# Two narrow attentions of a decoder joined into one pipeline of sixteen sequences

## The reference

```
self:   q = rope(x@Wq)  k = rope(x@Wk)  v = x@Wv     (8 key/value heads, each used by 4 heads)
        s = q.k, causal;  attn = softmax(s/4);  ctx = attn@v
        ctx = swapaxes(ctx,-2,-1).reshape(b,t,512);  x = layernorm(x + ctx@Wo)
cross:  q = axial_rope(x@Wq)  k,v = split(ctx_1024@Wkv);  k = axial_rope(k)     (32 key/value heads)
        attn = softmax(q.k/4);  x = layernorm(x + attn@v@Wout + bout)
```

## Time and profile before

| | us |
|---|---|
| median of 3 runs (4342.74 to 4356.64) | 4351.02 |
| the profiled execution | 4323.99 |
| its span, from first to last instruction | 4322.0 |
| mean granted TensorE clock, share of 2.4 GHz | 0.931 |
| TensorE matmul busy | 3714.3 (86%) |
| VectorE busy | 1918.8 (44%) |
| ScalarE busy | 1308.8 (30%) |
| self attention, narrow | from 2036 to about 2808 |
| cross attention, narrow | from about 2808 to about 3616 |

### The profile page before, as it was taken

The page is one execution under the profiler, slowest core; times in us unless marked ns, Lnnn a source line. Parts: engine busy times, 40 slices in busy tenths (PEclk is TensorE's granted clock), DMA queues, the critical chain, the costliest instruction groups (busy, mean ns, idle before and its releaser), DMA issues. The chain is left out here.

```text
span 4322.0 us, 60181 instructions
## 1 busy us (share of the span) xinstructions
PE 3714.3 (86%) x20058; PEld 2564.1 (59%) x20059; DVE 1918.8 (44%) x6611; ACT 1308.8 (30%) x2941; POOL 279.3 (6%) x304
## 2 busy tenths in 40 slices
PE   7899999899999998894688887768777886799996
PEld 7667777677777776542455554434444443577775
DVE  4334433344443443214454545545555555543435
ACT  1233322333333333411232333224333344221121
POOL 2231000030000000413000000000000000000000
PEclk8999999999999999897788999879999998899998
DMA  6511111131111111444000000010000001100001
GB/s 222 176 41 53 44 39 39 48 135 42 44 41 41 46 44 68 151 136 127 1 1 2 2 1 1 1 39 3 4 3 6 4 1 40 30 10 19 10 19 39
DMA packets 83735, 191.45 MB, mean 44 GB/s; under 512 B 22416, under 2 KB 27792, under 8 KB 82456
## 3 DMA queue, kind: packets, MB, share of 16 engines
q0 software_dynamic: 31360, 94.52, 7.1%
q1 hardware_dynamic: 52192, 94.53, 6.3%
HBM read 138.56 MB, written 50.47 MB: 44 GB/s over the span
## 5 line engine op out<-in xcount | busy, mean ns | idle before, releaser
L1696 ACT ACTIVATE probsT_c<-bank 128x512 f32<-128x512 f32 x256 | 147.5, 596 | 369.6 <-PE bank L1559 369.6
L1786 DVE TENSOR_REDUCE mx_y<-bank 128x2 f32<-128x512 f32 x288 | 185.9, 688 | 153.2 <-PE bank L1534 151.9
L1696 ACT ACTIVATE probsT_y<-bank 128x512 f32<-128x512 f32 x256 | 147.7, 596 | 312.6 <-PE bank L1552 310.0
L446 PE MATMUL bank<-wo_s,work_s 128*128 128x512 f32 x512 | 228.9, 598 | 7.1 <-ACT work_s L478 3.8
L446 PE MATMUL bank<-wo_x,work_x 128*128 128x512 f32 x512 | 227.2, 594 | 5.1 <-ACT work_x L478 3.8
L478 ACT ACTIVATE work_s<-bank 128x512 f32<-128x512 f32 (+1 forms) x224 | 104.2, 465 | 355.7 <-PE bank L435 174.4
L478 ACT ACTIVATE work_x<-bank 128x256 f32<-128x256 f32 (+1 forms) x240 | 109.6, 460 | 322.9 <-PE bank L435 188.6
L583 DVE CUSTOM_DVE_ANT_0 work_x<-bank,work_x 128x256 f32<-128x256 f32 x256 | 97.8, 420 | 221.0 <-issue 221.0
L524 ACT ACTIVATE work_x<-work_x 128x256 f32<-128x256 f32 x256 | 128.3, 502 | 195.9 <-DVE work_x L588 195.9
L583 DVE CUSTOM_DVE_ANT_0 work_s<-bank,const 128x128 f32<-128x128 f32 (+1 forms) x256 | 80.8, 353 | 214.3 <-issue 214.3
L1534 PE MATMUL bank<-kT_c,qT_c 64*128 64x256 f32 x576 | 91.2, 403 | 97.3 <-DVEq L1797 96.3
(11 more groups left out here) (416 smaller groups left out, 8195.4 us busy)
## 6 DMA issues: line engine op xcount, KB each, us to landing
wq_lo_s<-wq_lo_s POOLq DMA_DIRECT2D x64, 512.0 KB, 3.6
wq_lo_x<-wq_lo_x POOLq DMA_DIRECT2D x64, 512.0 KB, 3.5
expert_rows<-table_zero SPq DMA_DIRECT2D x20, 512.0 KB, 14.1
work_m<-expert_rows SPq DMA_DIRECT2D x40, 256.0 KB, 2.6
expert_products<-work_m POOLq DMA_DIRECT2D x40, 256.0 KB, 2.7
expert_table<-table_zero SPq DMA_DIRECT2D x16, 512.0 KB, 13.7
weights_m<-expert_table SPq DMA_DIRECT2D x4, 2048.0 KB, 9.8
ug_rows<-in_L_ffn_W_gate SPq DMA_DIRECT2D x9, 512.0 KB, 3.9
```

Of the source, the lines that this page charges most:

```text
L446: last = pe.matmul(out[t][:, :], oT[:, h, t * P:(t + 1) * P], wo[:, h, :], start=(h == 0), stop=(h == H - 1), skip_group_check=True)
L1696: act.activation(probsT[:, h % PTS, :], scoreT[h % 2][:, :], ACT.Exp, scale=SCALE)\
L1786: dve.tensor_reduce(mx[:, :, h], b[:, :].rearrange("p (t k) -> p t k", t=TILES), AX.X, ALU.max)\
```

## The change

The two calls become one. The 16 items are sequences 0 to 7 of the self attention and then 0 to 7 of the cross attention, written out without a loop (`ITEMS = 16`, `step(n, at)`).

- The finishing of item n-1 lies in the steps of item n: h0, h2 in step 0; h1, h3 in step 1; hT0, hT1 in step 3; out0 in step 8; out1 in step 9; bias, statistics, root and normalising in steps 10 to 13 (`norm_stage`). There is no tail between items.
- Item n+1 is prepared in steps 0 to 13 (k in 0 and 1, q in 4 and 5, v in 11 and 12), `xT` and `ctxT` of item n+2 in steps 14 and 15. `x_static` is gone: x is turned out of `x_all`. First scores lie in steps 8 to 15, two pairs each.
- The split is now high, low, high (or high, high, low): 48 rows of 64. The keys have ones in rows 48 and 49, and the negative maxima of the queries' rows (high and low) are written into rows 48 and 49 of `qT` by 8 small DMAs per item out of `negT` (negA for pairs 0 to 7, negB for 8 to 15). Second scores contract 50 rows; the matmuls with `select` are gone.
- For self, first scores of the first tile take 128 keys instead of 256, second scores of the second half 128 queries instead of 256, and the causal mask is added to the first scores by a bf16 matmul as well (2 more of 256 columns per pair). Maxima are one reduction per pair for both kinds: 128x768 for self, 128x1024 for cross.
- One exponential per pair (128x768 and 128x1024) instead of two of 128x512.
- Values of four heads at a time, in all four groups of 32 columns, at even steps; one bank for their result, three for `prep`.
- The cross weights are loaded on GpSimd's queue while self items run.

```diff
-        self.bank = [ctx.enter_context(nc.psum_tensor(f"bank{i}", [P, 512], FP32)) for i in range(8)]
+        self.banks = [ctx.enter_context(nc.psum_tensor(f"bank{i}", [P, 2, 512], FP32)) for i in range(4)]
+        self.bank = [self.banks[i // 2][:, i % 2, :] for i in range(8)]
...
+    def step(n, at):
+        f = n - 1 if n >= 1 else None
+        g = n + 1 if n + 1 < ITEMS else None
+        e = n + 2 if n + 2 < ITEMS else None
+        a, b = [], []
+        if f is not None:
+            a += {0: ["h0", "h2"], 1: ["h1", "h3"]}.get(at, [])
+            b += {3: ["hT0", "hT1"] if cross(f) else [], 8: ["out0"], 9: ["out1"]}.get(at, [])
+        a, b = [(x, f) for x in a], [(x, f) for x in b]
+        if at == 2:
+            a.append(("negB", n))
+        if g is not None:
+            whole = [x for x in ("kT02", "kT03", "kT12", "kT13") if cross(g)]
+            a += [(x, g) for x in {3: ["kT01"] + whole[0:1], 4: ["q0"] + whole[1:2], 5: ["kT11"] + whole[2:3],
+                                   6: ["qT00", "qT01"], 7: ["qT03", "qT10"], 10: ["qT12"], 11: ["v0"], 12: ["qT13"],
+                                   13: ["negA"]}.get(at, [])]
+            b += [(x, g) for x in {0: ["k0"], 1: ["k1"], 2: ["kT00"], 4: ["kT10"], 5: whole[3:4] + ["q1"], 6: ["qT02"],
+                                   7: ["qT11"], 12: ["v1"]}.get(at, [])]
+            if at >= 8:
+                a.insert(0, (2 * (at - 8), g))
+                b.insert(0, (2 * (at - 8) + 1, g))
...
+            for n in range(ITEMS):
+                for i, name in enumerate(("negA", "negB")):
+                    sp.wait_ge(s["prep_act"], uses.nth[name, n])
+                    for r in range(2):
+                        for l in range(2):
+                            row, at = 64 * r + ROWS + l, 16 * l + 8 * r
+                            sp.dma_start(qT[row:row + 1, n % 2, 8 * i:8 * i + 8, :].bitcast(FP32), negT[at:at + 8, i, :].bitcast(FP32))\
+                              .then_inc(s[f"{name}_there"], 16)
...
+            def second_scores(n, pair):
+                if pair % 8 == 0:
+                    pe.wait_ge(s["negA_there" if pair == 0 else "negB_there"], 64 * (n + 1))
+                pe.wait_ge(s["exp_ready"], n * PAIRS + pair)
+                for k in range(TILES):
+                    for h in (2 * pair, 2 * pair + 1):
+                        keys = kT[half(h, ROWS + 2), n % 2, key_block(n, h), k * P:(k + 1) * P]
+                        q0 = 0 if cross(n) else k * P
+                        last = pe.matmul(scoreT[:, h % 2, k * SEQ:(k + 1) * SEQ - q0], keys,
+                                         qT[half(h, ROWS + 2), n % 2, pair, q0:SEQ],
+                                         start=(k == 0), stop=cross(n), skip_group_check=True)
...
+            def values(n, quad):
...
+                for k in range(TILES):
+                    q0 = 0 if cross(n) else k * P
                     for i in range(4):
+                        h = 4 * quad + i
+                        kv = h if cross(n) else h // 4
+                        last = pe.matmul(hbank[VW * i:VW * (i + 1), col + q0:col + SEQ],
+                                         v[:, n % 2, k, VP * kv:VP * kv + VW],
...
+            for n in range(ITEMS):
+                for at in range(PAIRS):
+                    second_scores(n, at)
+                    early, late = step(n, at)
+                    for name, item in early:
+                        emit(name, item)
+                    if at == 0 and n >= 1:
+                        values(n - 1, 7)
+                    elif at >= 2 and at % 2 == 0:
+                        values(n, at // 2 - 1)
+                    for name, item in late:
+                        emit(name, item)
+            values(ITEMS - 1, 7)
+            for name, n in after:
+                emit(name, n)
```

More of the change, by code:

```diff
@@ L1301 @@
 NH, VW = 32, 32
[L1304 to L1340, removed]
@@ new lines, in read, with four, project @@
+            def read(name, n):
+                pe.wait_ge(s[f"prep_{uses.engine[name, n]}"], uses.nth[name, n])
+            def four(b, block):
+                for i in range(4):
+                    last = pe.transpose(b[:, P * i:P * (i + 1)], block(i), chip.ident)
+                return last
+            def project(b, src, t, w, width, chunks):
+                for cc in range(chunks):
+                    last = pe.matmul(b[:, 0:width], src[:, cc, t * P:(t + 1) * P], w[:, cc, :],
+                                     start=(cc == 0), stop=(cc == chunks - 1))
+                return last
@@ new lines, in finish @@
+                    last = four(b, lambda j: heads_n[:, j % 2, (2 * i + j // 2) * P:(2 * i + j // 2 + 1) * P])
+                else:
+                    if i == 0:
+                        read("hT1" if cross(n) else "h3", n)
+                        pe.wait_ge(s["wo_cross_loaded" if cross(n) else "wo_loaded"], 16)
+                    for j in range(DC):
+                        if cross(n):
+                            a = headsT[:, j, i * P:(i + 1) * P]
+                        else:
+                            a = heads_n[:, j % 2, 2 * i * P + j // 2:2 * (i + 1) * P:2]
+                        last = pe.matmul(b[:, :], a, wo[:, j, :], start=(j == 0), stop=(j == DC - 1))
@@ new lines, in keep_heads @@
+            def keep_heads(n, quad):
+                turn_ = n * 8 + quad
+                act.wait_ge(s["values_ready"], 4 * (turn_ + 1))
+                if n >= 1:
+                    act.wait_ge(s["prep_ready"], uses.ready["h2" if quad < 4 else "h3", n - 1])
+                col = turn_ % 2 * SEQ
+                copy(heads[:, quad, :], hbank[:, col:col + SEQ]).then_inc(s["heads_copied"], 1)
+            act.wait_ge(s["consts_ready"], 1)
+            for name, n in mine(before):
+                evacuate(name, n)
@@ new lines, in _ @@
+            for n in range(ITEMS):
+                for at in range(PAIRS):
+                    early, late = step(n, at)
+                    for name, item in early:
+                        do(name, item)
+                    if n >= 1 and at in (10, 11, 12, 13):
+                        norm_stage(at - 10, n - 1)
+                    for name, item in late:
+                        do(name, item)
+            for name, n in after:
+                do(name, n)
+            for part in range(4):
+                norm_stage(part, ITEMS - 1)
```

731 lines of the change are left out of this document (322 added, 409 removed).

## The result

| | before | after |
|---|---|---|
| median of 4 runs, us | 4352.95 (4342.74 to 4356.64) | 3948.45 (3942.04 to 3958.78) |
| profiled execution, us | 4323.99 | 3946.09 |
| mean granted clock | 0.931 | 0.933 |
| first second scores to the last output projection, us | 1504.2 | 1107.6 |

The ratio is 0.908 (95% interval 0.905 to 0.910). The change made the kernel 404 us faster; I had forecast 303. The sign was right, and 3948 lies inside the stated range of 3935 to 4150, but only because that range was stretched to take in the rival in which the clock stays up (3936).

The account below looks back on a forecast made before the run. It took TensorE's work and its waits, for maxima in late steps, as the bound. Prologue 70, self items of 74.5, cross items of 78.9 and the end summed to 1275 against 1577 us: 4048, own range 3990 to 4100, stated 3935 to 4150.

Parts of the forecast that it names:

- the rival in which the clock stays up: No clock loss in late steps: 16 x 7 = 112 us less than forecast, 3936; chance 0.18.
- the end of the bounds that I took: Values of four heads: 0.98 us (all side by side) to 1.96 (two by two); 0.98 taken.
- The estimate of 1.2 us: Time of a four-head values group by the skill's 2.38 times; would add some 1 to 2 us per item.
- the allowances: First halves, on top of spacings: 2 us waiting for VectorE's banks, 1.5 for small waits; 3.5 per item.
- The clock: Late steps mostly at 1.2 GHz: 3.5 us in hand-overs, 3.5 in the next item's start; 7 per item, bounds 0 to 14.
- The last item: Prepares nobody: 16 steps of about 2 us, four h, two outputs, a norm: 45 us.
- the periods: Sign named beforehand: an item takes 72 to 77 us in self and 76 to 81 in cross.
- The clock's sign: Sign named beforehand: clock of 0.5 to 0.7 in steps 10 to 15, higher in steps 2 to 9.
- The second filling: The 86.6 us between self and cross loops, called over a quarter of the 302 us saved.
- The new wait: Second scores waiting for negA's or negB's small DMAs, 6 to 12 us to landing: 0 to 2 per item, taken at 0.
- Carrying 27 us from profile to median: The median of runs lay 27 us above the profiled execution; added to 4022, it gives 4048.

Follow-up runs that it names:

- the halved maxima: Kernel after, with maxima taken over half of the keys of each tile (384 instead of 768 elements in self, 512 instead of 1024 in cross): ratio 0.877.

## Why the prediction was right, and where it was 100 us off

**What bounds the kernel.** Right: spacings and hand-overs, not busy shares. For the second halves the halved maxima show it.

**Prices of single groups.** Nearly all held: second scores 0.43 and 0.61 (forecast 0.43 and 0.63); a quad 1.00 and 0.79, the end of the bounds that I took; first pairs of cross 1.75 and of self 1.87 (both 1.8); no slowness of 48 or 50 rows or of 128 columns. Four tiles give 3.5 times (16 records of 0.22, the prediction's estimate, in 1.00). The estimate of 1.2 us that the prediction drew from the Trainium skill's 2.38 times for three (TensorE: Matmul & The Clock Gate, Packing small matmuls) is not what the trace has; scaled by 4/3, that figure would have given an estimate of 1.1.

**Places in the pipeline.** Item 0 is 9.1 us shorter than item 1 (58.5 against 67.6): forecast 9. Item 7 is 4.3 longer than items 1 to 6 on average (71.5 against 67.2): forecast 4. The end took 16.9 (forecast 17), the prologue, from 2056.1, 73.9 (forecast 70).

**First halves: the allowances.** This is the largest miss. The sum of spacings for self was 25.1, and items at full clock take 24.9 to 25.0. On it I had put 3.5 us (2 for VectorE's steps 0 and 1, 1.5 for small waits). The first halves hold 14.4 us of waiting in all, 0.9 per item, and more of it in cross. For cross it was 29.1 plus 3.5, against 30.5 at full clock in the kernel with halved maxima. 8 x 3.7 + 7 x 2.1 = 44 us.

**The clock.** Its direction was right, its extent not. I had put 3.5 us into the next item's first half, as if the kernel were slow through h, k and kT; the low stretch ends 5 us into the item, and first halves lose 1.0 in self and 1.6 in cross on average (25.9 against 24.9, 32.1 against 30.5). 8 x 2.5 + 7 x 1.9 = 33 us. Within the second half I had taken the lower level for most steps and spread 3.5 us over twelve hand-overs. In fact steps 10 to 13 of self take 17.0 us (forecast 18.3), at full clock where the windows above show it, and step 14 bears most of the loss, 7.0 where 3.6 were forecast and 4.1 to 4.4 are seen at full clock. That the sum came out right, 42.4, is luck: its parts did not.

**The last item.** 16 steps of about 2 with four h, two projections and a norm: 45 forecast, 34.9 measured to its last second scores; the steps take 1.65 and the projections hide the norm. 10 us.

44 + 33 + 10 are 87 of the 97 us between the forecast's 1205 for this stretch (1275 less 70) and 1107.6; the second halves hold another 8 (622 us for 630). The first rival (clock stays up, 3936) is nearest in time, but two thirds of those 97 us came from something else, so its nearness is luck too. Of the signs named beforehand the periods failed (65 to 69 in self, for 72 to 77; mostly 72 to 76 in cross, for 76 to 81), and they pointed at the halves at once. The clock's sign, 0.5 to 0.7 in steps 10 to 15, failed in self, where it is 1.00 up to step 13.

**"The second filling is over a quarter of that."** Wrong as a statement of worth, though the sum's own terms said so: by them breaking the pipeline costs 70 + 45 - 78.5 = 36, and 24 were measured. 86.6 us are gone from between the loops. But with the attentions apart the gap in the new form is 63.7 us, and item 7, which then prepares nobody, is 39.7 us shorter.

**The new wait.** Right at 0; its bounds of 6 to 12 us to landing were too high, it is 5.2 from turning to use, 2.8 of them the four issues. No row stood behind the 2 us that the prediction gave copy and issues.

**Carrying 27 us from profile to median.** Nothing in the rows said where they came from, but carrying them did little harm. The first profile of before (4323.99) lies where before's medians lie on three of the chips (4326 to 4329), and the medians of 4351 and 4353 are those of the slower side. The kernel after shows the same: 3930.30 in its repetition, 3948.45 as its median. Against the repetition the forecast without the 27 us, 4022, is 92 us off; with them, against the median, 100.

By stage, the 397 us of the stretch are 161 in the self items (694.2 to 533.3), 87 between the loops and 149 in the cross items (723.4 to 574.3). What the parts are worth, each undone alone: the end in one place 68, quads apart 58, maxima by matmul 24, the filling 24. They needn't add, and they leave over half of the 397 us to what wasn't undone: the form of the maxima, the masks, one exponential, the smaller k and v of self, x turned in place, the ninth sequence. By rows, first pairs of self fell from 2.18 to 1.87 and of cross from 1.89 to 1.75; how the rest divides was argued, not tried.

## What to carry to other kernels

For the first halves a sum of start-to-start spacings from the trace was right to 1% in self and 5% in cross; allowances put on top of it without a row of their own made almost half of the error, so give an allowance a row or leave it out. In a software pipeline look for the half in which one engine is the bound and move work of the other engine's kind there: moving the norm from beside the maxima into idle stretches of VectorE brought 1.6 us per item (24 / 15), and more once its last operations no longer stood in front of the next hand-over. Where the clock moves with the waiting, don't read a difference of 7 us in 1100 as the price of a part. And price joining two loops by the pipeline's own terms, filling minus what the drained item saves, not by the gap in the old timeline.

## What the runs showed of the hardware

- Two heads in 128x32 tiles take as long as four (0.98 and 1.00 us), also when the four are issued two by two (1.01), but not with other matmuls between them (58 us over the kernel).
- TensorE's clock fell to 1.2 GHz (0.51 granted) behind a stretch of 14 us in which it was 76% busy. Here a wait cost more than its length: 36 us of DMA waits made 51, and 64 us less of waiting gave 124.
- Four DMAs of 8 KB from SBUF into SBUF, gathered from 8 partitions onto one: 0.7 us each to issue, and 1.3 us from the end of the last issue to the first matmul that needs it (2125.82 + 2.80 to 2129.95).
- Behind the same expert part, the narrow stage's first turning of x came 9 to 33 us later in the four profiles taken beside the slower medians of before (2060.2 to 2070.1, against 2037.0 to 2051.0).
